# A decoder layer with routed experts on one core: who prepares the routing of the last batches, and when the first expert rows are loaded

## The reference

```python
x = x + self_attention(layernorm(x))          # 16 heads of 64
x = x + cross_attention(layernorm(x), ctx)    # 16 heads of 16, 361 keys a batch
x = x + ffn(layernorm(x))
# ffn: feats = layernorm(x); eid = argmax(feats @ centroids.T)       (8 experts)
#      xhat  = normalised feats; h = xhat * gamma[e] + beta[e]
#      y     = feats + relu(h @ w1[e] + b1[e]) @ w2[e] + b2[e]       (256 -> 1024 -> 256)
#      alpha = sigmoid(feats @ centroids[e]); out = alpha * y + (1 - alpha) * feats
```

## Time and profile before

| | us |
|---|---|
| three runs, median (lowest to highest) | 1566.71 (1562.39 to 1567.07) |
| the profiled execution | 1566.04 |
| its span, first to last instruction | 1564.3 |
| mean granted TensorE clock | 0.967 of full |

### The profile page before, as it was taken

One profiled execution on the slowest core, in us unless ns is written; L12 is line 12 of the kernel. 1 busy time (PEld: TensorE's weight loads), 2 busy tenths in 40 slices (PEclk: granted clock), 3 DMA queues, 4 the chain that ended last, 5 costly groups with the idle time before them and its releaser, 6 DMA issues. The chain is left out here.

```text
span 1564.3 us, 40213 instructions
## 1 busy us (share of the span) xinstructions
PE 1434.1 (92%) x12305; PEld 1241.7 (79%) x12305; DVE 967.4 (62%) x2473; ACT 763.7 (49%) x1879; POOL 682.0 (44%) x1060
## 2 busy tenths in 40 slices
PE   4999999999999999789999999999999369999997
PEld 3888878888888888668888888888887258888886
DVE  5747575757565656357777777777775235555553
ACT  4647474747464656236655655655655112222221
POOL 5434353535353535512355455465464523333332
PEclk9999999999999999789999999999999579999999
DMA  5606060707070707077667767767764235554451
GB/s 191 136 5 167 20 172 13 179 9 181 8 177 11 173 12 176 26 217 194 193 176 198 194 178 195 194 176 196 195 168 141 69 110 166 197 194 169 160 191 54
DMA packets 181964, 218.31 MB, mean 140 GB/s; under 512 B 83838, under 2 KB 150309, under 8 KB 181638
## 3 DMA queue, kind: packets, MB, share of 16 engines
q1 hardware_dynamic: 176360, 208.56, 48.1%
q0 software_dynamic: 3968, 6.59, 1.3%
q10 hardware_dynamic: 1568, 2.30, 0.5%
HBM read 138.67 MB, written 80.48 MB: 140 GB/s over the span
## 5 line engine op out<-in xcount | busy, mean ns | idle before, releaser
L1431 DVE TENSOR_REDUCE row_max<-psb_s 100x1 f32<-100x361 f32 x512 | 265.3, 530 | 140.1 <-PE psb_s L1654 135.0
L1305 ACT ACTIVATE probs<-psb_t 121x400 f32<-121x400 f32 (+1 forms) x384 | 190.4, 507 | 89.7 <-PE psb_t L1664 82.8
L1654 PE MATMUL psb_s<-k,q 97*100 97x362 f32 x512 | 185.0, 363 | 12.8 <-DVE row_max L1431 4.9
L519 POOL TENSOR_TENSOR diag<-neg_ident,row_max 100x400 fp32r<-100x400 f32 x128 | 112.8, 903 | 175.5 <-DVE row_max L612 146.7
L1664 PE MATMUL psb_t<-q,k 98*121 98x200 f32 (+1 forms) x768 | 148.5, 276 | 1.8 <-ACT probs L1305 1.8
L2144 PE MATMUL psd_h<-h_in,w_sb 128*128 128x256 f32 x640 | 144.0, 384 | 1.4 <-ACT h_in L2010 1.4
L2152 PE MATMUL psd_y<-w_sb,hid 128*128 128x256 f32 x640 | 144.5, 379 | 0.0
L2144 PEld LDWEIGHTS psd_h<-h_in,w_sb 128*128 128x128 f32 x640 | 123.3, 193 | 18.9 <-issue 1.8
L2152 PEld LDWEIGHTS psd_y<-w_sb,hid 128*128 128x128 f32 x640 | 120.1, 190 | 15.5
L1664 PEld LDWEIGHTS psb_t<-q,k 98*121 98x121 f32 (+1 forms) x768 | 126.8, 186 | 5.6 <-ACT probs L1305 2.5
L2025 ACT ACTIVATE hid<-psd_h,b_sb 128x256 f32<-128x256 f32 x100 | 47.4, 474 | 148.5 <-PE psd_h L2144 147.2
(11 more groups left out here) (230 smaller groups left out, 3710.0 us busy)
## 6 DMA issues: line engine op xcount, KB each, us to landing
w_sb<-in_w SPq DMA_DIRECT2D x40, 1024.0 KB, 7.6
routed_rows<-empty SPq DMA_DIRECT2D x7, 3855.0 KB, 18.7
packed_keys<-k_st SPq DMA_DIRECT2D x32, 724.0 KB, 4.1
k<-packed_keys SPq DMA_DIRECT2D x64, 362.0 KB
v_rows<-v_tok SPq DMA_DIRECT2D x32, 400.0 KB
v_ext<-v_rows SPq DMA_DIRECT2D x32, 400.0 KB
q<-packed_queries SPq DMA_DIRECT2D x64, 200.0 KB
k<-packed_keys SPq DMA_DIRECT2D x64, 181.0 KB
```

What stands on the lines that cost most here:

```text
L519: pool.tensor_tensor(diag[:, g % 2], c.neg_ident[0:S, 0:S].unsqueeze(1).to_broadcast([S, GH, S]), row_max[:, g // 2 % 2, g % 2].unsqueeze( ...
L1305: act.activation(probs[0:KT[kt], u % 2, kt], ps_t[i % 2][0:KT[kt], 0:4 * S], ACT.Exp, scale=HD2 ** -0.5).then_inc(probs_ready, 1)
L1431: dve.reduce_max(row_max[:, p, h:h + 1], ps_s[h % 2][0:S, 0:S2], AX_X).then_inc(max_ready, 1)
L1654: pe.matmul(ps_s[h % 2][0:S, 0:S2E], q2[0:97, p, u, g, S * a:S * (a + 1)], k2[0:97, p, u, g], start=True, stop=True).then_inc(scores_ready, 1)
```

## The change

- POOL no longer copies features or rows or works out slots for the last batches. It makes inverse roots for batches 30 and 31 (`routing_root`), adds counts, and sends rows of batches 27 to 31 straight from `c.x` (`send_last_rows`).
- VectorE makes the features of batches 30 and 31 (`last_features`) and the slots of batches 27 to 31 in four steps each (`last_places`).
- The rows buffer of the experts moves into `c.stage`, and SP loads tile 0's rows in the second block, after waiting for all sends, between the weights of tile 0 and those of tile 1.
- `add_counts` waits for the counts of the batch ahead.

```diff
@@ stage_for_cross_attention
+    ROWS_AT = 2192
+    c.rows = c.stage[:, ROWS_AT:ROWS_AT + 2 * (T // 128) * ROWW].rearrange("p (u t d) -> p u t d", u=2, d=ROWW)
...
@@ cross_attention, SP
             sp.wait_ge(c.tiles_ready, 2)
-            for j in range(2):
-                load_weights(sp, c, expert_of(sp, c, j), j, moe["w1"], moe["w2"])
+            load_weights(sp, c, expert_of(sp, c, 0), 0, moe["w1"], moe["w2"])
+            for p in range(2):
+                sp.wait_ge(routed[p], 16 * (B // 2))
+            load_rows_of(sp, c, 0, 0, xs)
+            load_weights(sp, c, expert_of(sp, c, 1), 1, moe["w1"], moe["w2"])
@@ cross_attention, POOL
             def add_counts(n, p):
                 pool.wait_ge(onehot_ready, n + 1)
+                reach(pool, counts_ready, n)
...
+            def send_last_rows(n):
+                pool.wait_ge(slot_ready, n + 1)
+                pool.indirect_dma_start(
+                    out=xs, out_offset=bass.IndirectOffsetOnAxis(ap=last_slots[:, n - (B - LAST):n - (B - LAST) + 1],
+                                                                 axis=0),
+                    in_=c.x[:, n, :], in_offset=None).then_inc(routed[n % 2], 16)
...
             over_batches(pool, step)
-            for b in range(B, B + 5):
-                routing(b, b % 2)
+            routing_root(B - 2)
+            add_counts(B - 4, 0)
+            send_last_rows(B - 5)
+            routing_root(B - 1)
+            for n in range(B - 3, B):
+                add_counts(n, n % 2)
+                send_last_rows(n - 1)
+            send_last_rows(B - 1)
@@ cross_attention, VectorE (LAST = 5)
+            def last_features(n):
+                dve.wait_ge(r_rstd_ready, n + 1)
+                dve.wait_ge(r_filled, n)
+                dve.tensor_scalar(feats[:], c.x[:, n, 0:D], r_mv[:, 0:1], r_rstd[:], ALU.subtract,
+                                  ALU.mult).then_inc(feats_ready, 1)
+            def last_places(n):
+                k, done = n - (B - LAST), 3 * (n - (B - LAST))
+                dve.wait_ge(r_copied, n + 3)
+                dve.tensor_tensor(place[:, 0], found[:, 1 - n % 2, 1], region[:], ALU.add).then_inc(last_placing, 1)
+                dve.wait_ge(last_placing, done + 1)
+                dve.tensor_tensor(place[:, 1], place[:, 0], onehot[:, n % 2].bitcast(F32), ALU.mult
+                                  ).then_inc(last_placing, 1)
+                dve.wait_ge(last_placing, done + 2)
+                dve.tensor_reduce(last_f[:], place[:, 1], AX_X, ALU.add).then_inc(last_placing, 1)
+                dve.wait_ge(last_placing, done + 3)
+                dve.tensor_copy(last_slots[:, k:k + 1], last_f[:]).then_inc(slot_ready, 1)
...
             for part in range(5):
                 choose(B - 4, 0, part)
             quotients(B - 1)
+            last_features(B - 2)
+            last_places(B - 5)
             residual(B - 1)
             route_stats(B - 1)
             route_moments(B - 1)
+            last_features(B - 1)
             for n in range(B - 3, B):
                 for part in range(5):
                     choose(n, n % 2, part)
+                last_places(n - 1)
+            last_places(B - 1)
             tiles()
@@ experts, SP
-            load_rows(0, 0)
```

More of the change, by code:

```diff
@@ L137, in stage_for_cross_attention @@
     c.bo_sb = take(D)[0:S]
+    ROWS_AT = 2192
+    c.rows = c.stage[:, ROWS_AT:ROWS_AT + 2 * (T // 128) * ROWW].rearrange("p (u t d) -> p u t d", u=2, d=ROWW)
+    c.rows_loaded = [ctx.enter_context(nc.semaphore(f"rows4_loaded{p}")) for p in range(2)]
     for name in ("w2_loaded", "mask_cleared", "mask_t_loaded", "mask_b_loaded", "key_mask_ready", "bias_ready",
@@ L827, in cross_attention @@
         KP = KT[0]
+        LAST = 5
         wq_sb, wk_st, wv_st, wo_sb = c.wq_sb, c.wk_st, c.wv_st, c.wo_sb
@@ L880, in cross_attention @@
         slot = sb("slot", [S, 2], U32)
+        last_f = sb("last_f", [S, 1])
+        last_slots = sb("last_slots", [S, LAST], U32)
         free = [0]
@@ L971, in cross_attention @@
         table = sem("table")
+        last_placing = sem("last_placing")
         K0, Q0, K1, MT1, RT, V0, MT0, V1, V2, XT = range(10)
@@ L1154, in live, with routing_root @@
                                  col.to_broadcast([KP, 3, H2])).then_inc(live_ready, 1)
-            def normalised_features(n):
+            def routing_root(n):
                 pool.wait_ge(r_mv_ready, n + 1)
@@ L1162, in normalised_features @@
                 pool.tensor_tensor(r_rstd[:], r_var[:], c.minus_half[0:S, 0:1], ALU.pow).then_inc(r_rstd_ready, 1)
+            def normalised_features(n):
+                routing_root(n)
                 pool.tensor_copy(row_in[:], at_batch(c.x, n, slice(0, D))).then_inc(row_ready, 1)
@@ L1860, in expert_of, with load_rows_of @@
                           else c.tile_expert[0:1, bass.ds(j, 1)], min_val=0, max_val=E - 1)
+def load_rows_of(sp, c, j, p, xs):
+    n = sp.value_load(c.tile_row[0:1, j:j + 1] if isinstance(j, int) else c.tile_row[0:1, bass.ds(j, 1)],
+                      min_val=0, max_val=E * MAXT)
+    src = xs.rearrange("(n t r) d -> n r t d", t=T // 128, r=128)[bass.ds(n, 1)].rearrange("o r t d -> r (o t) d")
+    sp.dma_start(c.rows[:, p], src).then_inc(c.rows_loaded[p], 16)
 def load_weights(sp, c, e, p, w1, w2):
@@ L1883, in experts @@
         HID_ACT, HID_DVE = (0, 2, 4, 6, 7), (1, 3, 5)
-        rows = sb("rows", [128, 2, NH, ROWW])
+        rows = c.rows
         stats = sb("stats4", [128, NH, 6])
@@ L1908, in experts @@
         pool_passed = c.pool_passed
-        rows_loaded = [sem(f"rows4_loaded{p}") for p in range(2)]
+        rows_loaded = c.rows_loaded
         stats_ready = sem("stats4_ready")
@@ L1947, in load_rows @@
                 reach(sp, token_ready, j - 1)
[L1948 to L1951, removed]
-            load_rows(0, 0)
+                load_rows_of(sp, c, j, p, xs)
             def load(j, p, last):
```

## The result

| | before | after |
|---|---|---|
| median of the runs beside the prediction (lowest to highest) | 1566.36 (1562.39 to 1567.07) | 1550.92 (1550.12 to 1551.95) |
| ratio | | 0.9911 [0.9897, 0.9926] |
| the profiled execution | 1566.04 | 1550.12 |
| its span | 1564.3 | 1548.4 |
| two later samples of after, 6 runs each, with 29 and 11 runs of before | 1564.27; 1563.70 | 1551.19; 1551.27 |

The change makes the kernel faster by 15.4 us in the first sample and by 13.1 and 12.4 in the two larger ones. The forecast was 10.5, and 1550.92 lies under the stated range.

The account below looks back on a forecast made before the run. TensorE bounds the loop and expert tiles; between them lies a 68 us hole where savings count fully. The tile table 4.9 us earlier and rows 10.4 after it give 10.5: 1566.71 - 10.5 = 1556.2, range 1552.5 to 1560.8 (80%).

Parts of the forecast that it names:

- Row load, T + 10.4: Tile 0's rows land 10.4 us after the tile table ends (16.0 before), 0.7 behind tile 0's weights.
- rival 2: Rows land with tile 1's weights, or the expert block starts late: about 5 us given back, 1561.2; 8%.
- the move alone is worth 5.6 us: Moving tile 0's row load between the two tiles' weights gains 5.6 us without any shortening of the routing tail.
- T + 4.5: A last send that meets weights lands near 4.5 us after the tile table ends, at no cost.
- What held the rows before: Before the expert tiles, send, landing, drain, block start, row load and preparation stand in series; a row load alone takes 3.0.
- Tail: In the last batches' routing, the tile table ends at 1237.85 instead of 1242.76, 4.9 us earlier.
- this is the step that pays: 4.0 us: VectorE ends the features of batch 31 at 1225.6 instead of POOL's 1229.6, 4.0 us earlier.
- The base: Summed against the profiled execution, 1566.04 us, 0.7 below the median of the runs, 1566.71, with the difference carried over.
- The lock of the shared port: Skill's rule: VectorE's lock on the shared SBUF port stops GpSimd writing DMA descriptors; by its factor 5.6 us a send, 1569.7.
- rival 3: Tail sends can't proceed during VectorE's SBUF steps; at 3.9 us per send the table moves by 11.7: 1567.9; 4%.
- Tiles, `add_counts`, stage buffer at nothing: Expert tiles unchanged, the added counts wait in the batch loop taken as 0, reuse of the stage buffer for rows 0.

Follow-up runs that it names:

- move alone: The kernel before, with only tile 0's row load moved between the weights of tiles 0 and 1: 1560.84 us, ratio 0.9982.
- tail alone: The kernel after, with tile 0's rows loaded at the start of the expert block as before: 1557.96 us, ratio 0.9964.
- before again: The kernel before, run again unchanged: 1563.68 us (1560.64 to 1568.31), ratio 1.0003.
- places on POOL: The kernel after, with POOL's old copy, six place steps and send put back, features staying on VectorE: 1559.5 us in one run.

## Why the prediction was wrong, step by step

- **Row load, T + 10.4.** Right: T + 10.2 (rows landed 1243.20), 0.7 behind the weights, so the rows kept their place, and VectorE started on them 0.1 us later, so no block start held them (both against rival 2). But "the move alone is worth 5.6 us" was wrong: it holds only together with the shorter tail. The T + 4.5 of a send that meets the weights counts on the send being issued 2.5 us before T, as in the new tail. With the old tail it is issued 2.3 us after T and by the earlier trace rows lands at T + 9.1, and the move alone shows the cost, 2.3 us. With the send out of the way this did not touch the sum.
- **What held the rows before.** Read in part only. The prediction put landing, drain, block start and load in series and took the 3.0 of the earlier trace rows as a load alone. The queue held the rows just as long: they landed 0.7 behind tile 1's weights. A block that starts 8 us sooner gained 0.2 in the tail alone. This did not touch the sum either, which took the landing from the weights.
- **Tail: this is the step that failed.** Forecast: T moves by 4.9, to 16.3 us after the last projection; measured 14.26, 14.14 and 13.86 in three traces, a gain of 7.0 to 7.4. Three durations were too long. I gave every send the 0.95 of start-up that the earlier trace rows show behind slots that POOL makes itself; behind slots made by VectorE it is 0.3, and root and features of batch 31 came 0.7 us earlier for it. The range had no bound for this term: its bounds end at a gain of 11.8. Places took 0.75 to 0.81 instead of 0.92, and `tiles` 3.76 instead of 3.94. And the counts of batch 31 were no longer held by send 29 (it ends 1227.53, the one-hot row 1227.55), where the schedule had 0.75 us of wait.
- **Which edit pays.** Wrong: "this is the step that pays: 4.0 us" was said of the features. Taken back alone they cost 1.9, the places 5.3 in T and 2.4 more at the send, in one trace each.
- **The base.** The sum was made against an execution that held a low-clock stretch of 3.9 us, and set against the median of the runs shown (1566.71). The larger samples put before at 1564.3 and 1563.7, 2.4 and 3.0 us under it, and leave after where it was (1551.2 and 1551.3). The range had an allowance of 2.4 us downward for the scatter of medians; single runs of before lie up to 11 us apart. It took both errors to leave the range: 10.5 off the larger samples gives 1553.2 to 1553.8, and 13 off the 1566.4 of the first gives 1553.4, both inside it.
- **The lock of the shared port.** Sends of the tail took 0.99 to 1.10 beside `choose` and places, no longer than before (1.04 to 1.12), so the hold that rival 3 needed isn't seen. The rule of the Trainium skill (SBUF — State Buffer, SBUF: two separate sides) is hardly tested by this: it names two-port modes of VectorE, and two SBUF inputs only against a GpSimd operation that reads SBUF, and the features (0.42), VectorE's only `tensor_scalar` over full rows in the tail, ran beside none of the sends (to 1222.12, between sends that end at 1220.69 and start at 1224.28).
- **Tiles, `add_counts`, stage buffer at nothing.** Nothing speaks against it: 296.0 against 296.4 us behind the first expert matmul. Up to the last score matmul after took 1202.0, 1199.5 and 1199.0 us in three traces and before 1200.9 and 1199.6, so a cost of the wait in the loop would be within the scatter of 3 us.

Together: 10.5 forecast, + 2.1 to 2.5 in the tail, + 0.2 in the row load, is 12.8 to 13.2, and the larger samples show 13.1 and 12.4. The other 2.4 of the first sample is which executions it drew, luck and not an effect of the change.

## What to carry to other kernels

Behind a serial tail, write each interval from a fixed event and compare these, not end times: a clock that falls in some executions moved one interval, the last step, by 3.0 to 3.9 us in either kernel. Put on a queue first what the longest chain waits for, not what is ready first; 257 KB behind 2 MB cost 6.2 us, half of what the whole change gained. A wait taken off a chain gains nothing while a second one ends at the same time; look for it before pricing the first. And let another engine make the last thing that a send of POOL waits for: in these traces that saved 0.6 us a send.

## What the runs showed of the hardware

- POOL's indirect send of 100 rows lands in 2.7 to 2.9 us in the tail while SP's queue is idle, and in 6.4 to 6.8 beside weight transfers on it (before, before again, move alone, places on POOL).
- It starts 0.88 to 1.00 us (1.13 at the first send of each run) after a result of POOL's own that it waits for, 0.31 to 0.34 after one of VectorE's, and 0.21 behind an operation of POOL that it doesn't wait for.
- POOL's DRAIN at the end of the block took 2.68 us in both kernels, begun 0.2 us after the last send had landed; it was hidden in after. In before it lay on the chain of waits, but the queue held the rows as long.
- Matmuls with zeros held the granted clock at the high level for 17.5 us. A pause of 1.4 us behind them was followed by 3.4 us at the low one in one trace and by none in two. In the last step they did not keep the low level away: one of three traces spent 13.7 us at it.
- The same program spread over 11 us (1559.2 to 1570.0 in 29 runs), and its mean clock from 0.974 to 0.964 at the two ends.
